# Offsets of a planned instruction order searched anew, with the plan's transfer costs changed

## What is computed

```
h = layernorm(x) * (1 + ca) + sa
x = x + ga * attention0(h)                       # softmax(q k^T * scale) v, 16 heads
h = layernorm(x) * (1 + cb) + sb
x = x + gb * (sum over the 2 best of 8 experts of comb * swiglu_e(h) + swiglu_shared(h))
h = layernorm(x) * (1 + ca') + sa'
x = x + ga' * attention1(h)                      # causal
h = layernorm(x) * (1 + cb') + sb'
x = x + gb' * (sum over the 2 best of 8 experts of comb * relu(h W1_e)^2 W2_e)
```

## Time and profile before

| what | before |
|---|---|
| median of 3 runs (lowest to highest) | 1106.16 us (1104.87 to 1110.31) |
| the profiled execution, its time | 1110.95 us |
| its span, from the first to the last instruction | 1109.2 us |
| TensorE busy (matmul) | 1006.2 us, 91% |
| VectorE busy | 855.4 us, 77% |
| ScalarE busy | 723.6 us, 65% |
| GpSimd busy | 441.3 us, 40% |
| mean granted clock of TensorE | 0.942 of full |
| moved by the DMA engines | 176.06 MB, 159 GB/s |

### The profile page before, as it was taken

How to read it: one execution, slowest core, us unless ns; L and a number is a source line. 1 busy time by engine, 2 the same in 40 slices (tenths; PEclk the granted TensorE clock), 3 DMA queues, 4 the chain that set the end, 5 groups by cost and what they waited for, 6 DMA issues and landing times. The chain is left out here.

```text
span 1109.2 us, 22558 instructions
## 1 busy us (share of the span) xinstructions
PE 1006.2 (91%) x8299; PEld 539.3 (49%) x8299; DVE 855.4 (77%) x1746; ACT 723.6 (65%) x1144; POOL 441.3 (40%) x536
## 2 busy tenths in 40 slices
PE   4588898899999999999999998899999888999986
PEld 3122122224555454555566665566666554455554
DVE  3799989878988889887767886689786476877365
ACT  4058687668666786767676664676564786776863
POOL 3002022245012535620473533673331375746463
PEclk9569899989999999999999999899898998999998
DMA  4814253355746695656468675678775656511110
GB/s 132 183 32 126 66 161 90 107 177 172 216 150 192 199 268 144 203 152 193 152 219 254 200 206 188 202 189 266 216 244 158 201 157 172 128 62 57 67 30 20
DMA packets 122510, 176.06 MB, mean 159 GB/s; under 512 B 20281, under 2 KB 86201, under 8 KB 122401
## 3 DMA queue, kind: packets, MB, share of 16 engines
q1 hardware_dynamic: 116064, 161.24, 49.6%
q0 software_dynamic: 5760, 12.59, 3.9%
q10 hardware_dynamic: 576, 0.79, 0.3%
HBM read 114.77 MB, written 59.67 MB: 157 GB/s over the span
## 5 line engine op out<-in xcount | busy, mean ns | idle before, releaser
L1001 DVE TENSOR_REDUCE nm<-ps 128x2 f32<-128x1024 f32 (+3 forms) x512 | 504.5, 1017 | 96.8 <-PE ps L775 49.9
L1338 ACT ACTIVATE ES<-ps 128x1024 f32<-128x1024 f32 (+1 forms) x448 | 418.9, 962 | 124.8 <-PE ps L792 63.5
L809 PE MATMUL ps<-ES,VS 128*9 128x512 f32 (+3 forms) x2048 | 227.9, 533 | 0.8 <-DVE hdx L1175 0.4
L770 PE MATMUL ps<-KS,QS 48*128 48x512 bf16 (+3 forms) x1024 | 180.1, 371 | 38.7 <-DVE nm L1001 20.0
L792 PE MATMUL ps<-QS,KS 51*128 51x512 bf16 (+3 forms) x1024 | 171.2, 353 | 16.6 <-ACT ES L1338 5.8
L870 PE MATMUL ps<-hsT,wst 128*128 128x128 f32 x1104 | 158.9, 289 | 6.7 <-DMA wst<-we 3.9
L870 PEld LDWEIGHTS ps<-hsT,wst 128*128 128x128 f32 x1104 | 137.1, 196 | 45.9 <-issue 35.1
L770 PEld LDWEIGHTS ps<-KS,QS 48*128 48x128 bf16 x1024 | 50.0, 96 | 153.4 <-DVE nm L1001 57.0
L792 PEld LDWEIGHTS ps<-QS,KS 51*128 51x128 bf16 x1024 | 50.0, 94 | 152.8 <-issue 50.8
L1557 POOL DMA_INDIRECT gr<-d_y,pos x80 | 83.6, 1045 | 90.9 <-DMA gr<-d_y,pos 46.9
L1487 POOL TENSOR_TENSOR nmp<-nmr,nmp 32x128 bf16<-32x128 f32 x32 | 13.5, 422 | 168.2 <-ACT nmp L1330 167.8
(11 more groups left out here) (199 smaller groups left out, 1457.7 us busy)
## 6 DMA issues: line engine op xcount, KB each, us to landing
wst<-we SPq DMA_DIRECT2D x92, 576.0 KB
d_u<-US SPq DMA_DIRECT2D x64, 256.0 KB
KS<-d_k SPq DMA_DIRECT2D x64, 192.0 KB
QS<-d_q SPq DMA_DIRECT2D x64, 192.0 KB
hs<-d_h SPq DMA_DIRECT2D x25, 256.0 KB
d_y<-ys SPq DMA_DIRECT2D x25, 256.0 KB
d_q<-sp SPq DMA_DIRECT2D x16, 384.0 KB
d_k<-sp SPq DMA_DIRECT2D x16, 384.0 KB
```

The lines of the kernel that those rows point to most:

```text
L770: mm = eng.matmul(psum[:, bank[u][a], c:c + n], QS[m][r:r + KA, pr, 128 * t1:128 * t1 + 128], KS[m][r:r + KA, pr, 0:n], start=True, stop=i ...
L809: mm = eng.matmul(psum[32 * a:32 * a + 9, b, q0:S], VS[i % 3][:, j1, 4 * g + a, :], ES[(2 * EXP[i, g, j] + a // 2) % NES][:, a % 2, c:c + ...
L1001: ins = eng.tensor_reduce(nm[f][:, :].rearrange("p (a c) -> p a c", a=2)[:, :, 4 * pr + t1], ps2("score", i, f, pr, t)[:, :, c:c + n], AX. ...
L1338: eng.activation(ES[(2 * n + pp) % NES][:, :, 0:w], ps2("bscore", i, f, g, j, pp)[:, :, 0:w], ACT.Exp, scale=SC1 if i >= NB else SC0).then ...
```

## The change

No instruction is added or taken away. The plan's costs change, and the whole table of offsets is another. In settle(), a step on POOL that needs a transfer becomes ready 0.65 us later (WAKE), PIPE goes from 1.3 to 1.0, and five short transfers are named in MOVES. Many lags of transfers are changed. The weights of steps on TensorE stay what they are, and nothing in settle() follows the clock.

```diff
@@ the table (one row of each kind; all others change in the same way)
-LAST = {"bscore": -0.01, "c": 5.84, "d": 3.15, "expo": -4.85, "f": 2.77, "g": -4.33, "ld": -1.68, "m": 6.33, "max": -9.12, "p": -1.4, "pv": -0.02, "r": -16.14, "rowmax": -0.94, "rr": -2.57, "s": -3.38, "score": -0.01, "stack": -2.39, "t": -7.19, "u": -0.1, "w": -6.08, "x": 2.04}
+LAST = {"c": 7.34, "d": 4.1, "expo": 0.0, "f": 7.32, "g": -22.08, "ld": 4.31, "m": 2.19, "max": -7.66, "p": -7.32, "pv": -5.43, "r": -16.63, "rowmax": 2.4, "rr": 4.34, "s": -1.76, "score": -0.01, "stack": 9.09, "t": -12.61, "u": -0.35, "w": -4.19, "x": -6.22}
...
-    "s": [-0.34, 5.69, 0.01, 0.36, -9.7, -0.13, 0.13, 0.12, 11.35, 25.39, 2.53, 1.37, 8.4, -24.24, -18.6, -8.24],
+    "s": [1.0, -0.11, -2.44, 0.35, -10.35, -4.82, -0.01, 0.09, 13.96, 20.32, 4.15, 4.7, 23.03, -33.38, -31.12, -15.13],
...
@@ MOVES
-             "x_w": 2.0, "c_h": 3.2, "ld": 1.0, "r_sc": 0.27, "g_ga": 0.27, "d_out": 1.0}
+             "x_w": 2.0, "c_h": 3.2, "ld": 1.0, "r_sc": 0.27, "g_ga": 0.27, "d_out": 1.0, "max_st": 0.25, "max_ld": 0.5,
+             "t_st": 0.15, "g_gc": 0.4, "m_st": 0.1}
...
@@ settle()
-                ready[n] = max(ready[n], end + lag)
+                woken = WAKE if k[0] in self.MOVES and self.work[n][0] == "POOL" else 0.0
+                ready[n] = max(ready[n], end + lag + woken)
...
-PIPE = 1.3
+PIPE, WAKE = 1.0, 0.65
```

More of the change, by code:

```diff
@@ L77 @@
[L77 removed]
+SHIFT = {"bscore": -0.08, "c": -25.68, "d": 1.2, "expo": -2.72, "f": 0.83, "g": -5.86, "ld": -29.52, "m": 7.71, "max": -0.32, "p": -0.35, "pv": 0.21, "r": 7.07, "rr": -0.96, "s": 0.48, "score": -0.08, "stack": -0.42, "t": -1.12, "u": 8.76, "w": 0.14, "x": 1.09}
@@ L263, in plan @@
     for b in range(2, NB):
-        load(f"x{b}", b - 1.0, 5.0, after=[("stack", b - 1, 1)])
+        load(f"x{b}", b - 1.0, 2.9, after=[("stack", b - 1, 1)])
     for n, name in enumerate(("bo", "c1", "fs")):
-        load(name, 1.0 + 0.1 * n, 4.0, after=[("stack", 1, 1)])
+        load(name, 1.0 + 0.1 * n, 2.9, after=[("stack", 1, 1)])
     add("POOL", ("c_more", 0), 5.5, 0.0, [("p_lo", 0, 1)])
@@ L315, in plan @@
             add("SP", ("stack", i, f), 2.1, i + 0.2 + 0.1 * f,
-                [("p_store", i, n, c) for n in range(2) for c in range(3)] + [("bscore", i - 2, f, 1, KEYS[i - 2][-1], 1)], lag=3.4)
+                [("p_store", i, n, c) for n in range(2) for c in range(3)] + [("bscore", i - 2, f, 1, KEYS[i - 2][-1], 1)], lag=4.7)
         for f in range(2):
@@ L354, in plan @@
             add("ACT", ("u_copy", i, g), 0.49, u + 0.1, [("pv", i, g, KEYS[i][-1]), ("u_st", i - (g < 2), (g - 2) % NG)], closes=[("pv", i, g, 0)])
-            add("SP", ("u_st", i, g), 0.4, u + 0.1, [("u_copy", i, g)], lag=2.4)
+            add("SP", ("u_st", i, g), 0.4, u + 0.1, [("u_copy", i, g)], lag=2.1)
         u = i + 2.05
-        add("SP", ("u_ld", i), 1.2, u, [("u_st", i, g) for g in range(NG)] + [("t_rc", i - 1), ("t_mm", i - 1)], lag=3.0)
+        add("SP", ("u_ld", i), 1.2, u, [("u_st", i, g) for g in range(NG)] + [("t_rc", i - 1), ("t_mm", i - 1)], lag=3.1)
         add("DVE", ("t_rc", i), 0.47, u, [("u_ld", i), ("t_st", i - 1)])
-        add("SP", ("t_st", i), 0.4, u, [("t_rc", i)], lag=1.2)
-        add("SP", ("t_ld", i), 0.6, u, [("t_st", i), ("t_o", i - 1)], lag=2.8)
-        add("SP", ("t_gt", i), 0.5, u - 0.5, [("m_st", l)] + ([("s_x", i - 2), ("r_hx", i - 2), ("t_add", i - 2), ("d_x", i - 2)] if i < N - 1 else [("s_dn", NB - 1)]), lag=4.0)
+        add("SP", ("t_st", i), 0.4, u, [("t_rc", i)], lag=1.4)
+        add("SP", ("t_ld", i), 0.6, u, [("t_st", i), ("t_o", i - 1)], lag=2.55)
+        add("SP", ("t_gt", i), 0.5, u - 0.5, [("m_st", l)] + ([("s_x", i - 2), ("r_hx", i - 2), ("t_add", i - 2), ("d_x", i - 2)] if i < N - 1 else [("s_dn", NB - 1)]), lag=2.9)
         add("DVE", ("t_o", i), 0.61, u, [("t_ld", i)])
@@ L410, in plan @@
                     add("POOL", ("r_sc", q, t, c), 1.35, u, [sent[-2], ("rr_pos", q), ("r_hx", first + t // NT), ("c_h", (max(MT) - 1) // 12)]
-                        + [("x_ld", q - 1, L) for L in range(XL[q - 1] if q else 0)], lag=2.1)
+                        + [("x_ld", q - 1, L) for L in range(XL[q - 1] if q else 0)], lag=1.35)
                     sent.append(("r_sc", q, t, c))
```

43 lines of the change are left out of this document (21 added, 22 removed), and 16 rows, old and new, of the table NUDGE.

## The result

The change made the kernel slightly slower, where I had forecast 0.8% faster.

The account below looks back on a forecast made before the run. TensorE, busy 1006.2 of 1109.2 us, bounds the kernel, so only idle time and half clock can be won. Terms: 3.6 + 3.1 + 3.0 + 1.7 + 2.0 - 4.4 = 9.0 us, median 1097 us, range 1081 to 1114.

Parts of the forecast that it names:

- Term 1 and 2: Stall of 3.61 us before batch 13's first recomputed score, second half, goes: 3.6 us; the clock fall behind it: 3.1 us.
- Term 3: Stall of 3.07 us at 686.92 us, on weights of expert tile 22, group 2, goes: 3.0 us; its clock fall: 1.7.
- Term 4: Batch 1's shared feed-forward step "s_dn", at 243.30 us, comes 13 scores earlier, where there is idle time: 2.0 us gained.
- Term 5: All other moved steps may uncover waits on ACT and DVE, 4.4 us each with a clock fall: -4.4 us.
- the full stretch: From 234.15 to 640.34 us, TensorE 12.2 us idle at clock 1.00: the change cannot earn there, though it can lose.
- SP's wait for the gains of batch 9: Rival: near 680 us SP waits on this load ("t_gt"), making the expert weights behind it late; slower, 1114 us, chance 0.17.
- No net gain: Rival: the two priced stalls go, but three more of 4.4 us come elsewhere; 1106 us, chance 0.28.
- The third rival: Stalls on ACT and DVE thin out too, with half the remaining falls and idle time gone; 1077 us, chance 0.10.
- The condition that I had set for being wrong: Sign in the new profile: the forecast is wrong if new stalls above 1.7 us number more than three.

Follow-up runs that it names:

- ab236: The order of the change up to the first score of i = 4 (236 us), then that of the kernel before: 1100.02 us, ratio 0.9907 to before.

## Why the prediction was wrong

I gave faster by over 0.5% a chance of 0.53, slower 0.17; the median of 1113 lies within the range, near its upper end.

- **Term 1 and 2, the stall at 934 us and its fall (3.6 + 3.1).** The stall went, as forecast: a wait on the maxima ("QS <- d_m") of 1.7 to 3.7 us stands in all nine kernels with before's order there, and in none of the three with that of the change.
- **Term 3, tile 22 and its fall (3.0 + 1.7).** The stall went too, but it was priced too high. The 3.07 us are one draw: the longest wait on "wst" behind 640 us in the eight other kernels with before's order there is 0.6 to 1.9 us. In the same way part of the rise of the clock in the fourth stretch, from 0.93 to 0.99, is before's slow draw. What the last part as a whole is worth is open: -0.04% by the sums with t equal in both directions, up to -0.99% without.
- **Term 4, "s_dn" of batch 1.** It came at 220.97 us, still 2.05 us long. The 2.0 us that I gave to the second stretch were far too few: this part gained 11.7 us, and the clock's share is 8.5 to 12.7. I had computed 14 us of loss from that clock in the first section, and then priced one step instead.
- **Term 5, all other moves (-4.4).** This is the step that failed, and with it the sentence on the full stretch: I wrote that the change "can lose there", and gave it nothing to lose. The middle part lost 18.8 us or more by the splices, and by the sum of steps in the trace of after some 20 to 24 us by 620 us: 4.8 and 4.6 in its two holes, 7.4 between 580 and 620, the rest spread. The prediction said that "the trace has no row for this" and took single stalls on ACT and DVE and their falls, 4.4 us each, as nearest. Those rows were of the wrong kind: up to 340 us the loss is 10.5 us more of idle time, most of it in waits of 0.2 to 0.9 us, and 10.2 us at half clock. Before's trace gives a warning, though no size: TensorE is idle for 12.2 of 406.19 us in the full stretch, so what it loses there to such waits it has no room to make up.
- **The rivals.** SP's wait for the gains of batch 9 did not become a stall; no wait on "wst" stands among those of the fourth stretch of after. So the result was slower for another reason than the one to which I gave 0.17, and that it lies in the range, up to that rival's 1114, is luck. "No net gain" was right in its form (gains in one place, new waits in others) and off by the size. The third rival has a true point: the clock did rise, though the plan has no clock. Its mean was 0.954 over the 20 runs of after, and 0.944 to 0.945 over the runs of before beside the experiments. It was outweighed.
- **The condition that I had set for being wrong** ("if new stalls above 1.7 us number more than three") was met by four: 2.44 us at 243.50, 2.69, 2.19 and 2.61 us in the fourth stretch. They are the smaller part of the loss.

The Trainium skill (page "TensorE: Matmul & The Clock Gate", section "What's actually happening") says that the ramp penalty is under 1% of a typical kernel's span. Counted over all falls, as the prediction did, this kernel does not agree: the clock of before's profile stands at half for 129.7 of 1109 us. TensorE is busy for 95 us of them, so some 47 us are lost, 4% of the span, and 33 us without the stretch at the start.

What stays open: what in the first 173 us lifts the clock; the price of a splice at 652 us in each direction, and with it what the last part is worth; whether the third hole, from 580 to 600 us, is the cause of the loss there; and whether a missing kind or mere lateness makes the hand-made holes so dear.

## What to carry to other kernels

Where one engine is full and every piece of its work leans on a helper (here VectorE for scores, ScalarE for second scores, neither for experts), look at an order as a mix, by counting each kind in windows of 20 us, and not as a list of stalls: two edits that left a kind out for 16 us cost 1.6 to 1.8% each, with no wait over 1.4 us to point at. When a planner's costs and its table change together, put both orders under the same costs first; here that says "no gain" at once, though it does not rank differences under 1%. When you splice, give each cut a kernel with the opposite passage too, because the passage has a price of its own. And when an order is another throughout, splice the two at a few steps: the best part of a change that loses may well be kept, as ab236 keeps 0.9%.
